# The closing pass of a graph convolution made inside its loop over edges

## The reference, cut to what matters

```
def gcn_conv(x, src, dst, W, b):
    deg = segment_sum(ones_like(src), dst);  dinv = where(deg > 0, rsqrt(deg), 0)
    msg = (x @ W)[src] * (dinv[src] * dinv[dst])[:, None]
    return segment_sum(msg, dst) + b
src, dst = add_self_loops(edge_index, n)
h   = relu(gcn_conv(relu(layernorm(x)), src, dst, W1, b1))   # 64 -> 32
out = x + gcn_conv(h, src, dst, W2, b2)                      # 32 -> 64
```

## Time and profile before

| | us |
|---|---|
| median of 3 runs | 7210.75 |
| the profiled execution | 7213.7 |
| its span, first to last instruction | 7211.8 |
| gc2: gathers' start to last add's start | 6505.84 to 7038.54 |
| closing pass: first scale to last instruction | 7040.57 to 7211.8 |

### The profile page before, as it was taken

The page is one execution under the profiler, slowest core; times in us unless marked ns, Lnnn a source line. Parts: engine busy times, 40 slices in busy tenths (PEclk is TensorE's granted clock), DMA queues, the critical chain, the costliest instruction groups (busy, mean ns, idle before and its releaser), DMA issues. The chain is left out here.

```text
span 7211.8 us, 108709 instructions
## 1 busy us (share of the span) xinstructions
PE 4767.5 (66%) x33408; PEld 4265.9 (59%) x33408; DVE 4774.0 (66%) x6428; ACT 1735.7 (24%) x2361; POOL 3426.2 (48%) x2958
## 2 busy tenths in 40 slices
PE   4666334770278786555554888887678784784797
PEld 2355334660178785555554878886568774673675
DVE  5999544225677786666666965557798783782458
ACT  0044112330144343222222431112244550000001
POOL 0099665771277402777773017650000007766766
PEclk8966667995599898766766999999999997997999
DMA  5198666768722375223232767778757983112009
GB/s 227 23 273 266 158 145 141 143 139 329 277 74 75 90 247 171 77 80 80 78 79 63 242 227 243 243 239 257 235 198 249 327 315 105 52 58 90 14 12 285
DMA packets 891168, 1194.07 MB, mean 166 GB/s; under 512 B 546145, under 2 KB 629686, under 8 KB 889598
## 3 DMA queue, kind: packets, MB, share of 16 engines
q1 hardware_dynamic: 565198, 859.74, 36.8%
q10 hardware_dynamic: 193840, 251.55, 10.2%
q0 software_dynamic: 131712, 77.25, 7.5%
HBM read 736.76 MB, written 457.73 MB: 166 GB/s over the span
## 5 line engine op out<-in xcount | busy, mean ns | idle before, releaser
L914 POOL DMA_INDIRECT gc_msgs<-t,src_rows x784 | 753.3, 961 | 1401.9 <-POOLq L150 1109.7
L2322 PEld LDWEIGHTS gc_ring<-gc_msgs,gc_hot 128*128 128x128 f32 x4736 | 621.4, 208 | 311.2 <-issue 304.1
L2322 PE MATMUL gc_ring<-gc_msgs,gc_hot 128*128 x4736 | 648.5, 295 | 235.8 <-SPq L2281 234.9
L968 POOL DMA_INDIRECT acc<-de_sums,de_put x392 | 607.0, 1548 | 314.9 <-issue 159.4
L914 POOL DMA_INDIRECT at1s_ends<-x,src_rows x392 | 395.6, 1009 | 492.1 <-POOLq L150 372.9
L1102 PE MATMUL de_ring<-de_win,de_pick 128*128 x2368 | 342.2, 305 | 265.2 <-DMA de_win<-t 265.2
L1102 PEld LDWEIGHTS de_ring<-de_win,de_pick 128*128 128x128 f32 x2368 | 322.6, 217 | 286.3 <-issue 281.2
L914 POOL DMA_INDIRECT at1s_ends<-x,dst_rows x392 | 419.1, 1069 | 119.4 <-issue 119.4
L914 POOL DMA_INDIRECT re_rows<-x,src_rows x392 | 406.7, 1037 | 125.1 <-issue 124.8
L914 POOL DMA_INDIRECT at2s_ends<-h,src_rows x392 | 374.0, 954 | 180.2 <-issue 114.6
L1470 PE MATMUL re_psR<-w_rel,re_own 128*128 128x128 f32 x3136 | 403.6, 295 | 72.8 <-DVE re_own L1407 72.5
(11 more groups left out here) (498 smaller groups left out, 11801.4 us busy)
## 6 DMA issues: line engine op xcount, KB each, us to landing
rew_win<-x SPq DMA_DIRECT2D x74, 544.0 KB, 4.0
at1w_win<-g SPq DMA_DIRECT2D x74, 544.0 KB, 4.0
at2w_win<-g SPq DMA_DIRECT2D x74, 544.0 KB, 4.0
de_near<-same SPq DMA_DIRECT2D x74, 512.0 KB, 5.2
de_win<-t SPq DMA_DIRECT2D x74, 512.0 KB, 4.4
x<-rew_win SPq DMA_DIRECT2D x74, 512.0 KB, 2.9
h<-at1w_win SPq DMA_DIRECT2D x74, 512.0 KB, 2.8
h<-at2w_win SPq DMA_DIRECT2D x74, 512.0 KB, 2.9
```

The source lines that it names most:

```text
L914: nc.gpsimd.indirect_dma_start(buf[:, t * width:(t + 1) * width], None, table, bass.IndirectOffsetOnAxis(ap=rows[:, t:t + 1], axis=0)).the ...
L968: nc.gpsimd.indirect_dma_start(g.acc0[j % SUMS], bass.IndirectOffsetOnAxis(ap=put[:, j:j + 1], axis=0), sums[:, j * D:(j + 1) * D], None, ...
L2322: done = nc.tensor.matmul(ring[:, bass.ds(to[n], SLOT)], hot[k][:, n, :], each_group(msgs[:, bass.ds(of[n], MID)], SLOT // MID), start=Fal ...
```

## The change

The closing pass is made inside gc2. `gcn_last` takes the place of gc2's `gcn_edges` and of `gcn_close`. When a block's adds are done, the 16 node tiles behind the staircase's edge get no more edges, and they are scaled, turned, multiplied, added to x and stored in the next blocks' time: 74 closings of 16 tiles (windows that overlap while the staircase hardly moves over the nodes), where `gcn_close` had 49.

A block is cut in two units of 8 steps. `hot` is made per unit (four buffers), and the ring is two buffers of one unit. ACT clears a ring buffer by a copy of zeros (1024 columns) and lays the bias into `psH` by a copy of 1024 columns ahead of the product, which then accumulates on it. POOL makes only gathers. x is loaded and `out` stored by ACT's queue, with three x buffers. `out` is written in the kernel's own layout (4 KB pieces in place of 256 B pieces) and reordered after the launch. Setup makes a second table of columns (`halves`) and two more columns of `blocks`, with six small DVE instructions.

```diff
-            gcn_edges(nc, g, "gc2", g.t4, acc, None)
-            gcn_close(nc, g, acc, out)
+            gcn_last(nc, g, g.t4, acc, out)
...
+            @block.scalar
+            def _(act):
...
+                act.wait_ge(blanked, 1)
+                load(1)
+                load(2)
+                clear(0)
+                clear(1)
+                for m in range(BLOCKS + 1):
+                    if m >= 1:
+                        turn(m)
+                    if m + 1 < BLOCKS:
+                        clear(2 * m + 2)
+                    if m >= 1:
+                        bias(m)
+                    if m + 1 < BLOCKS:
+                        clear(2 * m + 3)
+                    if m >= 2:
+                        store(m - 1)
+                        if m + 1 <= BLOCKS:
+                            load(m + 1)
...
+                def clear(unit):
+                    if unit >= 2:
+                        act.wait_ge(added, unit - 1)
+                    nc.scalar.activation(ring[:, unit % 2 * BUF:(unit % 2 + 1) * BUF], blank[:, :], ACT.Copy).then_inc(zeroed, 1)
...
+                def bias(m):
+                    if m >= 2:
+                        act.wait_ge(ready, m - 1)
+                    nc.scalar.activation(grouped(psH[:, :], D), each_group(g.w["bg2"][:, :], S), ACT.Copy).then_inc(biased, 1)
...
+            @block.tensor
+            def _(pe):
+                def turn(m):
+                    pe.wait_ge(scaled, m)
+                    if m >= 2:
+                        pe.wait_ge(evac, m - 1)
+                    transpose_pairs(nc, psT, u[m % 2], g.ident, S // 4).then_inc(turned, 1)
+
+                def widen(m):
+                    pe.wait_ge(evac, m)
+                    pe.wait_ge(biased, m)
+                    times(nc, psH, uT[m % 2], g.w["gcn2"], S // 4, start=False).then_inc(product, 1)
+
+                for m in range(BLOCKS):
+                    regs = [nc.tensor.alloc_register(f"gc2_step{m}_{n}") for n in range(S)]
+                    nc.tensor.load(regs, g.steps[m:m + 1, 0:S])
...
+                    nc.tensor.load(slots, g.halves[m:m + 1, 0:S])
...
+                    need = pe.value_load(g.blocks[m:m + 1, 1:2], min_val=1, max_val=STEPS)
+                    pe.wait_ge(arrived, need)
+                    for n in range(S):
+                        unit = 2 * m + n // HALF
+                        if n % HALF == 0:
+                            pe.wait_ge(hot_made, unit + 1)
+                            pe.wait_ge(zeroed, unit + 1)
+                        done = nc.tensor.matmul(ring[:, bass.ds(to[n], SLOT)], hot[unit % 4][:, n % HALF, :],
...
+                        if n % HALF == HALF - 1:
+                            done.then_inc(summed, 1)
+                            if m >= 1 and n < HALF:
+                                turn(m)
+                    if m >= 1:
+                        widen(m)
+                turn(BLOCKS)
+                widen(BLOCKS)
...
+            @block.vector
+            def _(dve):
...
+                for m in range(BLOCKS):
+                    add(2 * m)
+                    if m >= 2:
+                        close(m - 1)
+                    if 2 * m + 3 < 2 * BLOCKS:
+                        compare(2 * m + 3)
+                    add(2 * m + 1)
+                    scale(m + 1)
+                    if 2 * m + 4 < 2 * BLOCKS:
+                        compare(2 * m + 4)
+                close(BLOCKS - 1)
+                close(BLOCKS)
```

More of the change, by code:

```diff
@@ L248, in build @@
         g.steps = keep("steps", [P, 3 * S], i32)
-        g.blocks = keep("blocks", [P, 6], i32)
+        g.blocks = keep("blocks", [P, 8], i32)
+        g.halves = keep("halves", [P, S], i32)
         setw(g, "gcn2", keep("w_gcn2", [P, 4 * D]))
@@ L500, in _ @@
                 v.tensor_scalar(g.steps[:, S:2 * S], at[:, :], turn[:, :], odd[:, :], ALU.mult, ALU.add)
+                link(v.tensor_scalar(half[:, 0:HALF], at[:, 0:HALF], float(SLOT), None, ALU.mult))
+                link(v.tensor_scalar(half[:, HALF:S], at[:, HALF:S], at[:, HALF:HALF + 1], None, ALU.subtract))
+                link(v.tensor_scalar(half[:, HALF:S], half[:, HALF:S], float(SLOT), float(HALF * SLOT), ALU.mult, ALU.add))
+                v.tensor_copy(g.halves[:, :], half[:, :])
+                v.tensor_scalar(g.blocks[:, 6:7], node[:, HALF:HALF + 1], float(MID), None, ALU.mult)
                 link(v.tensor_scalar(ahead[:, :], edge[:, :], edge[:, 0:1], None, ALU.subtract))
@@ L2365, in _, with gcn_last @@
                         nc.vector.scalar_tensor_tensor(grouped(o[:, :], MID), grouped(o[:, :], MID), 0.0, dinv, ALU.max, ALU.mult).then_inc(done_made, 1)
[L2368 to L2380, removed]
-        with nc.Block() as block:
+def gcn_last(nc, g, nodes, acc, out):
+    W = B * MID
+    BUF = HALF * SLOT
+    with Room(nc, g, "gc2") as r:
+        msgs = r.sb("msgs", [P, T * MID])
+        hot = [r.sb(f"hot{k}", [P, HALF, P]) for k in range(4)]
+        blank = r.sb("blank", [P, BUF])
+        x = [r.sb(f"x{k}", [P, S * D]) for k in range(3)]
+        u, uT = ([r.sb(f"{n}{k}", [P, S * MID]) for k in range(2)] for n in ("u", "uT"))
+        ring, fixed = r.ps("ring", [P, 2 * BUF]), r.ps("fixed", [P, 512])
+        psT, psH = r.ps("psT", [P, S * MID]), r.ps("psH", [P, S * D])
+        got = [r.sem(f"got{k}") for k in range(4)]
+        x_in = [r.sem(f"x_in{k}") for k in range(3)]
+        acc_in, done_out = r.sem("acc_in"), r.sem("done_out")
+        arrived, blanked, hot_made, zeroed, summed, added, link_s, scaled, turned, evac, product, ready, biased = (r.sem(n) for n in (
+            "arrived", "blanked", "hot_made", "cleared", "summed", "added", "link", "scaled", "turned", "evac", "product", "ready", "biased"))
+        with nc.Block() as block:
+            @block.gpsimd
+            def _(pool):
+                for b in range(STEPS):
+                    if b >= 4:
+                        held(pool, arrived, b - 3, g.passed)
+                    gather(nc, msgs[:, b * W:(b + 1) * W], nodes, g.src_rows[:, b * B:(b + 1) * B], got[b % 4])
@@ L2382, in _ @@
             @block.sync
             def _(sp):
[L2384 to L2389, removed]
+                for k in range(4):
+                    part = slice(k * (PITCH // 4) * MID, (k + 1) * (PITCH // 4) * MID)
+                    sp.dma_start(acc[:, part], nodes.rearrange("(p t) d -> p (t d)", t=PITCH)[:, part]).then_inc(acc_in, 16)
@@ L2391, in _ @@
             @block.vector
             def _(dve):
[L2393 to L2431, removed]
-                    else:
[L2433 to L2447, removed]
+                v = nc.vector
+                link = Link(dve, link_s)
+                v.memset(blank[:, :], 0.0).then_inc(blanked, 1)
@@ new lines, in _, with compare, add @@
+                link(v.tensor_copy(fixed[:, 0:P], g.across[:, :]))
+                def compare(unit):
+                    if unit >= 4:
+                        dve.wait_ge(summed, unit - 3)
+                    v.tensor_tensor(hot[unit % 4][:, :, :], each_group(fixed[:, 0:P], HALF), spread(g.steep[:, unit * HALF:(unit + 1) * HALF], P),
+                                    ALU.is_equal).then_inc(hot_made, 1)
+                def add(unit):
+                    at = nc.vector.alloc_register(f"gc2_at{unit}")
+                    nc.vector.load(at, g.blocks[unit // 2:unit // 2 + 1, 6:7] if unit % 2 else g.blocks[unit // 2:unit // 2 + 1, 0:1])
+                    window = acc[:, bass.ds(dve.snap(at, donate=True, min_val=0, max_val=(TILES - 1) * MID), HALF * MID)]
+                    dve.wait_ge(summed, unit + 1)
+                    if unit >= 1:
+                        dve.wait_ge(added, unit)
+                    if unit >= 2:
+                        dve.wait_ge(scaled, unit // 2)
+                    v.tensor_tensor(grouped(window, MID), grouped(window, MID),
+                                    grouped(ring[:, unit % 2 * BUF:(unit % 2 + 1) * BUF], SLOT)[:, :, 0:MID], ALU.add).then_inc(added, 1)
@@ new lines, in scale @@
+                def scale(m):
+                    if m < BLOCKS:
+                        regs = [nc.vector.alloc_register(f"gc2_end{m}_{n}") for n in range(2)]
+                        nc.vector.load(regs, g.blocks[m:m + 1, 2:4])
+                        first = dve.snap(regs[0], donate=True, min_val=0, max_val=TILES - S)
+                        ended = acc[:, bass.ds(dve.snap(regs[1], donate=True, min_val=0, max_val=(TILES - S) * MID), S * MID)]
+                        dinv = spread(g.dinv[:, bass.ds(first, S)], MID)
+                    else:
+                        ended = acc[:, (TILES - S) * MID:TILES * MID]
+                        dinv = spread(g.dinv[:, TILES - S:TILES], MID)
+                    dve.wait_ge(added, 2 * m)
+                    if m >= 3:
+                        dve.wait_ge(turned, m - 2)
```

(16 more changed lines are left out.)

37 lines of the change are left out of this document (34 added, 3 removed).

## The result

| | before | after |
|---|---|---|
| median, us | 7210.24 | 7329.2 (7324.51 to 7338.32) |
| span of the profiled execution | 7211.8 | 7329.9 |
| first step of block 11 | 6666.86 | 6676.74 |
| last edge block's first step | 7034.36 | 7311.36 |

The ratio is 1.0165, 95% interval 1.0150 to 1.0179: slower by 119 us. The forecast was 37 us, to 7247, with a range up to 7325. The direction was right and the size was wrong by a factor of three.

The account below looks back on a forecast made before the run. TensorE bounds late blocks, gathers early ones, transfers the closing. Block 11 at 6666.9, 62 periods of 9.09 (563.6), 16.7 at the end and 0.9 setup give a span of 7248.1, about 7247 us as median; range 7185 to 7325.

Parts of the forecast that it names:

- What bounds, and what leaves: Last two stages: transfers bound the closing pass, 172.6 us that leave the end; TensorE bounds late blocks, gathers early ones.
- up to some 11 us is covered: Early blocks, whose adds are 11.85 us apart: waiting for gathers hides added work of up to some 11 us a block.
- The chain of a block: Late block, first step to next first step: 4.98 + 0.40 + 1.10 + 1.85 + 0.76 = 9.09 us.
- `widen`'s release: Late block on TensorE: the closing's product is released by ScalarE's bias 4.98 us after the block's first step.
- Dispatch: TensorE's sequencer: issuing the product's four matmuls ahead of the register loads takes 0.40 us, an estimate.
- the second load: TensorE's second load of 16 registers, behind the product: taken as stretched near a store, 1.85 us against 1.10 undisturbed.
- Slow clock: TensorE in late blocks: idling brings 1.2 GHz, first unit 0.96 longer, period 10.05 us, time 7307; chance 10%.
- the end behind block 73's start: End of the kernel: from the last block's start, its product, the last closing and the store take 16.7 us.
- the 0.9 of setup: Kernel setup: six more instructions of 0.15 us each add 0.9 us.
- Loads undisturbed: TensorE's register loads in late blocks: not stretched by the store, period 8.34 us, time 7201; chance 15%.
- Loads hidden: TensorE's sequencer in late blocks: loads run while the product waits, period 6.81 us, time about 7106; chance 17%.
- The row of ScalarE that spoke against it: Trace before the change: ScalarE's register load began at 4101.7, just when the waiting clear ahead started at 4101.66.

Follow-up runs that it names:

- the fillers: The changed kernel plus two float32 matmuls of 512 columns, read by nobody, behind each `widen` (the closing's product): 7275.2 us, ratio 1.0089.
- the small store: The changed kernel with only the first 64 of 1024 columns of each closing stored to `out`: 7211.26 us, ratio 1.0009.
- the exchanged waits: The changed kernel with only `widen`'s two waits, for `evac` and `biased`, in the opposite order: 7332.71 us, ratio 1.0160.
- the kernel with the bias first: The changed kernel with DVE's closing ahead of the first unit's add and ScalarE's bias ahead of the turned sums' copy: 7114.1 us, ratio 0.9860.

## Why the prediction was wrong

*What bounds, and what leaves*: right for the late blocks. The closing pass left the end, transfers and gathers did not bound late blocks, DVE and ScalarE are busy less than half of the time. For the early blocks, "up to some 11 us is covered" was too wide: the 11.85 is a mean with two gaps of 20 us in it, the other blocks lay about 10 apart, and blocks of 10 to 12.5 fell behind the gathers.

*The chain of a block*: right link by link. `widen`'s release 5.12 for 4.98, the loads behind it, one of the two stretched by the store. Dispatch was forecast 0.40 and took less than 0.1 (the load starts with `widen`); the second load was forecast 1.85 and took 2.09. In blocks at full clock the period is 9.39 for 9.09.

*Slow clock*: this is the step that failed. The prediction gave it 10% and set it aside because "both idle times are below 2.54", from one row in which a unit behind 2.54 of idle time ran at full clock. In the trace after, first units behind 2.48 and 2.17 are fast and one behind 2.21 is slow: the length of one idle stretch does not decide. In its place the runs showed 33 of the 62 late blocks with a slow first unit, their periods 10.98 for 9.39, and 54 us less with the idle time filled. The rival's own numbers, T = 10.05 and 7307 against 10.24 and 7329, were near by luck in part: it had 0.96 more for every block, and it was 1.59 more for about half of them.

The difference to the forecast's span, 81.8 us (118.1 measured, 36.3 forecast), adds up: 33 slow blocks x (10.98 - 9.39) = 52.5; block 11 later by 9.9, of which 4.3 are later and slower gathers and 5.6 the blocks' lag behind them (with the fillers, whose register loads are as long, the lag is 0.5, so about 5 of it is the slow clock); 62 x (9.39 - 9.09) = 18.6 for loads and links; the end behind block 73's start, 18.5 for 16.7, 1.8; less the 0.9 of setup, which is in block 11's start already. The clock has about 58 of the 81.8. The range ended at 7325 because it allowed the slow clock only a quarter of a microsecond over its own estimate and the early blocks nothing.

*Loads undisturbed*: the small store showed its price, 7211 for 7201. *Loads hidden*: its mechanism does not hold here, its size does. With the loads out of the path by other means the kernel takes 7131 or 7114, where the rival had 7106. The row of ScalarE that spoke against it, a load begun when the clear ahead was released, was the right one to go by; but the prediction gave the hold to the separate wait instruction, and the exchanged waits showed that `widen`'s matmuls do it too while the first of them waits.

The Trainium skill (Perfetto Trace Analysis, section "Per-engine timelines", tensor engine instruction) says that the sequencer is ready for the next instruction once a waiting matmul is pushed. The runs do not show that for the loads here: with one waiting matmul ahead, four records of which the first waits, the load began at 7319.4, as the matmul did at 7319.41. Whether the waiting record alone would have let it pass stays open. What agrees is that matmuls which wait for nothing are pushed ahead of their execution, by 0.8 us in the kernel with the bias first.

What stays open: what in a block's pattern of work and idle time decides between the two levels, and why the slow unit comes mostly in every other block. The runs show only that 0.85 + 2.2 us idle in 9.4 loses the full clock and 0.85 + 1.4 in 8.4, with the small store, keeps it.

## What to carry to other kernels

When a separate stage is folded into a loop, follow the new wait on each engine's sequencer: here it delayed not only the instruction but every register load behind it. Here the order of two instructions on ScalarE and DVE decided between 1.6% slower and 1.4% faster. And when a loop gets idle time on TensorE that it did not have, price the lower clock for the units behind it, on all of them, instead of excluding it by one fast row.

## What the runs showed of the hardware

Matmuls of which the first waited on a semaphore kept the register loads behind them from starting, four of them (7225.17 and 7225.2) and also one alone (7319.41 and 7319.4), while matmuls that were only queued did not (loads 0.8 us ahead). A load of 16 registers took 1.13 undisturbed and 2.09 in the median when begun some 0.6 us after a 512 KB store was issued (0.31 to 0.93); with a store of 32 KB it kept 1.13. TensorE's granted clock was 0.55 in the slow first unit shown; 33 of 62 blocks, idle 3 us of 9.4, had one (3.08 to 3.68 us for 2.05). It stayed at 1.00 when 0.95 us of matmuls that nobody reads were put into the gap.
